# Graph network on one core: in the SAGE rounds, TensorE signals its consumers from drains instead of from the last transpose or product

## What is computed

```python
# block 0: two SAGE layers with normalised rows; block 1: four SAGE layers
agg = segment_sum(h[src], dst); mean = agg / max(count(dst), 1)
h = relu(norm(mean @ W_l + b_l + h @ W_r))      # block 0
h = relu(mean @ W_l + h @ W_r + b)              # block 1
x = layernorm(x + h)                            # after each block
# block 2: attention by edge (GAT); block 3: transformer attention, batch norm
dst = minimum(100000 * uniform ** 2, 99999), sorted
```

## Time and profile before

| what | value |
|---|---|
| median of three executions | 14006.47 us |
| profiled execution, first to last instruction (span) | 16848.3 us |
| mean granted TensorE clock in the profiled execution | 0.667 of full speed |
| TensorE products busy | 8724.5 us, 52% |
| TensorE weight loads busy | 6051.7 us, 36% |
| VectorE busy | 7447.1 us, 44% |
| ScalarE busy | 4895.5 us, 29% |
| GpSimd busy | 7480.4 us, 44% |

### The profile page before, as it was taken

The page is one execution under the profiler, slowest core; times in us unless marked ns, Lnnn a source line. Parts: engine busy times, 40 slices in busy tenths (PEclk is TensorE's granted clock), DMA queues, the critical chain, the costliest instruction groups (busy, mean ns, idle before and its releaser), DMA issues. The chain is left out here.

```text
span 16848.3 us, 221135 instructions
## 1 busy us (share of the span) xinstructions
PE 8724.5 (52%) x38799; PEld 6051.7 (36%) x38898; DVE 7447.1 (44%) x21114; ACT 4895.5 (29%) x11500; POOL 7480.4 (44%) x7460
## 2 busy tenths in 40 slices
PE   6654344533344455445545544454544446677765
PEld 2121233422333344334434433343333323344444
DVE  6654234424454122121112113447888864444456
ACT  0000122223444122122212213344555541222257
POOL 2545554354322654554465455433334336554410
PEclk9775566756666566566656766666666667777776
DMA  6000234424443245345424534554333331233367
GB/s 253 1 3 1 75 120 139 156 71 125 135 143 121 87 148 171 94 126 159 152 88 148 171 97 143 169 190 147 120 121 119 120 113 47 79 98 110 118 193 245
DMA packets 1169327, 2072.17 MB, mean 123 GB/s; under 512 B 283810, under 2 KB 292531, under 8 KB 1156371
## 3 DMA queue, kind: packets, MB, share of 16 engines
q1 hardware_dynamic: 662400, 1128.29, 22.2%
q10 hardware_dynamic: 268534, 564.37, 8.7%
q0 software_dynamic: 238336, 378.92, 8.3%
HBM read 1358.91 MB, written 773.68 MB: 127 GB/s over the span
## 5 line engine op out<-in xcount | busy, mean ns | idle before, releaser
L639 POOL DMA_INDIRECT agg<-y_rows,s_idx x3136 | 3246.2, 1035 | 5507.4 <-ACT y_rows L970 2718.8
L883 PE MATMUL o_bank<-b_parts,ones_parts 3*128 3x512 bf16 (+1 forms) x1568 | 786.2, 501 | 3838.8 <-ACT h_t L1043 2893.0
L886 PE MATMUL o_bank<-w_r,h_t 128*128 128x128 f32 x12544 | 2587.7, 370 | 0.0
L1594 DVE TENSOR_TENSOR total<-o_bank,agg_in 128x512 f32<-128x512 f32 (+1 forms) x1568 | 1048.1, 688 | 3377.2 <-DMA agg_in<-agg 2068.9
L886 PEld LDWEIGHTS o_bank<-w_r,h_t 128*128 128x128 f32 x12544 | 2204.2, 264 | 536.9 <-issue 536.2
L1043 ACT ACTIVATE h_t<-ht_bank 128x512 f32<-128x512 f32 (+1 forms) x1568 | 878.3, 594 | 3930.8 <-remote 2694.1
L883 PEld LDWEIGHTS o_bank<-b_parts,ones_parts 3*128 3x128 bf16 (+1 forms) x1568 | 148.9, 95 | 4192.2 <-ACT h_t L1043 3123.9
L970 ACT ACTIVATE y_rows<-edge_bank,inv 128x128 f32<-128x128 f32 x2352 | 658.7, 373 | 2807.7 <-remote 1640.9
L789 PE MATMUL edge_bank<-w_l,run 128*128 128x128 f32 x4704 | 962.0, 383 | 951.7 <-DVE run L1410 776.4
L630 POOL DMA_INDIRECT gath<-node_a,g_idx x1176 | 1124.9, 957 | 513.6 <-issue 355.1
L630 POOL DMA_INDIRECT gath<-node_x,g_idx x784 | 780.1, 995 | 1079.4 <-PE edge_bank L829 646.1
(11 more groups left out here) (257 smaller groups left out, 14785.5 us busy)
## 6 DMA issues: line engine op xcount, KB each, us to landing
agg_in<-agg SPq DMA_DIRECT2D x1560, 256.0 KB
node_a<-h_out ACTq DMA_DIRECT2D x780, 256.0 KB
h_in<-node_a SPq DMA_DIRECT2D x780, 256.0 KB
node_x<-h_out ACTq DMA_DIRECT2D x392, 256.0 KB
node_b<-h_out ACTq DMA_DIRECT2D x392, 256.0 KB
h_in<-node_x SPq DMA_DIRECT2D x390, 256.0 KB
h_in<-node_b SPq DMA_DIRECT2D x390, 256.0 KB
agg<-zeros ACTq DMA_DIRECT2D x96, 1024.0 KB
```

The costliest lines, as they stand in the source:

```text
L639: pool.indirect_dma_start(agg[order(r)], bass.IndirectOffsetOnAxis(s_idx[q][:, k:k + 1], 0), y_rows[q][:, k, :], None, bounds_check=N - 1, ...
L883: pe.matmul(o_bank[s][0:p, :], ones_parts[:, 0:p], b_parts[:, r, :].unsqueeze(1).to_broadcast([3, RPP, P]), start=True, stop=False, skip_g ...
L886: last = pe.matmul(o_bank[s][0:p, j * P:(j + 1) * P], h_t[s][:, j, 0:p], w_r[r][:], start=False, stop=j == RPP - 1, skip_group_check=True)
L1594: dve.tensor_tensor(flat(total[s], p), o_bank[s][0:p, :], flat(agg_in[s], p), ALU.add).then_inc(sum_ready[s], 1)
```

## The change

In the SAGE rounds the four kinds of TensorE groups (L781, L789, L877 with L886) no longer increment their semaphore with the last transpose or product. A `drain` follows the group, and the drain increments the same semaphore by the same amount. In `front`, which GAT and TR share, the drain is taken only where the kind of the round is SAGE. The short description of the change also says that GpSimd issues all its DMAs without breaks; the diff edits nothing in GpSimd's stream.

```diff
                     for k in range(CPB):
-                        last = pe.transpose(pe_bank[q][:, k * P:(k + 1) * P], gath[q][:, k, :], ident[:])
-                    last.then_inc(gt_ready[q], 1)
+                        pe.transpose(pe_bank[q][:, k * P:(k + 1) * P], gath[q][:, k, :], ident[:])
+                    pe.drain().then_inc(gt_ready[q], 1)
...
-                            last = pe.matmul(pe_bank[2 + q][:, k * P:(k + 1) * P], run[q][:, k * P:(k + 1) * P],
-                                             w_l[r][:], start=True, stop=True, skip_group_check=True)
-                        last.then_inc(yp_ready[q], 1)
+                            pe.matmul(pe_bank[2 + q][:, k * P:(k + 1) * P], run[q][:, k * P:(k + 1) * P],
+                                      w_l[r][:], start=True, stop=True, skip_group_check=True)
+                        pe.drain().then_inc(yp_ready[q], 1)
...
-                        last.then_inc(htp_ready[s], 1)
+                        if kind == SAGE:
+                            pe.drain().then_inc(htp_ready[s], 1)
+                        else:
+                            last.then_inc(htp_ready[s], 1)
...
-                        last.then_inc(mm_ready[s], 1)
+                        if kind == SAGE:
+                            pe.drain().then_inc(mm_ready[s], 1)
+                        else:
+                            last.then_inc(mm_ready[s], 1)
```

More of the change, by code:

```diff
@@ L866, in tr_pair, with front @@
                         tr_values(i + 1, 0)
-                def front(u, r=r, tail=tail):
+                def front(u, r=r, tail=tail, kind=kind):
                     for s in range(2):
```

## The result

The changed kernel takes 15568.38 us (median of 4 executions, 15544.67 to 15590.32), the kernel before in the same measurement 13999.94 us (4 executions, 13985.01 to 14007.88). The ratio is 1.1122 with the interval 1.1106 to 1.1138: slower by 1568 us. The sign is the one forecast, but 14250 and the range up to 14700 are missed by far.

A forecast was written before the change was run, and what follows sets the result against it. No engine is busy above 52%, so waits decide: GpSimd's bursts set the first 35 pairs, units the last 14. Bubbles of 225 us in five rounds and 15 in round 1 make 14006 + 240 = 14246, rounded 14250; range 13880 to 14700.

The forecast's parts named there:

- Two loads that a pair puts side by side: Plain SAGE round: a pair costs the larger of GpSimd's 20.6 us burst and its units; 1130 us a round.
- I therefore take the late signals to be mostly a matter of the recorded execution: TensorE's signals, 15 us late during GpSimd bursts, explain about 2000 of 2842 us between profiled and timed; timed kernel nearly free.
- The bubble: Behind each drained TensorE group the next group moves by 0.35 us (0 to 0.9); 3528 drains, 1235 us on the engine.
- Half on the path: Where units set the pair's time, half of four bubbles counts: 0.7 us a unit, 35 us a round, pairs 10 more.
- TensorE has slack: First 35 pairs, set by GpSimd's bursts: 744 us of TensorE work in over 1000 a round, so nothing charged.
- The clock: TensorE: gaps may lower its clock, product groups then 2.05 us; used only against the lower bubble, no term in the sum.
- the way to 5%: Sign: a timed kernel 5% slower would mean a drain costs far more than a bubble or the clock fell.
- Late signals avoided: Rival, 0.18: TensorE's late signals are real in timed runs and drains go round them; 13750 us or less.
- a span near 15000: Sign in the profile after: span near 15000 us, "remote" before h_t, y_rows and total gone in rounds 0 to 5.
- Lateness inherited: Rival, 0.08: completion itself is late, so TensorE stands still behind drains, idle 10 us and more; 14750 us.
- Nothing measurable: Rival, 0.12: bubbles fall where TensorE waits anyway; only the signal's delay costs, 20 us in all; 14026 us.
- GpSimd "without breaks": GpSimd's instructions are unchanged and it already issues without breaks, 0.30 us between DMAs; this half costs nothing.

The follow-up runs named there:

- own waits: Against the changed kernel: no drains; the last instruction increments and TensorE waits for that increment at all four places; 15136.56 us, ratio 1.0824 to the kernel before.
- units only: Against the changed kernel: drains only behind the h_in transposes and the products with w_r, none on the edges' groups; 18008.95 us, ratio 1.0672 to the kernel before.
- the bare drain: Against the changed kernel: increments back on the last instruction, a drain that signals nothing behind it, all four places; 18610.3 us, ratio 1.1037 to the kernel before.

## Why the prediction missed

**Two loads that a pair puts side by side, the last 14 to 17 pairs set by units: right.** Without late signals the first third runs at GpSimd's pace, 319 us for 16 pairs, changed or not, with own waits or with drains behind the h transposes alone; a plain round takes 1122 us where I had worked out 1130.

**"I therefore take the late signals to be mostly a matter of the recorded execution": wrong.** Timed and profiled executions of one chip agree: a median of 16856.61 us goes with a span of 16862.8 on one, 13989.15 with 13999.1 on another. The page of before and the times shown with it came from chips in different conditions, so the 2842 us between them say nothing of the recording. By luck the consequence was right, since the chip where the result was timed has none: late signals play no part in the ratio.

**The bubble: size about right.** I took 0.35 us for the move of the next group. The rows show gaps of 0.23, 0.32, 0.23 and 0.70 us, 0.37 on the mean, behind the end of a group; with the 0.06 to 0.17 us by which groups overlapped before, the move is nearer 0.5, within my bounds of 0 and 0.9. The load stands behind the end of the group, by 0.20 us in the row shown, as expected. What I had not foreseen is the 0.70 us behind the last group of a unit. It is there with own waits too (0.61 us), so it isn't the drain's. The profile shows no other engine's wait there; the engine's own loop work is my guess and wasn't tested.

**"Half on the path" and "TensorE has slack" in the first 35 pairs: wrong from pair 17 on.** In the second third I charged nothing, and it lost 84 us. In the last third and the tail I charged 45 us, and it lost 229. Units went from 6 to 7 us to 8.84, and I had said about 6.

**The clock: the step that failed.** I wrote "Gaps may lower it" and used that only against the lower bubble, with no term in the sum. It is nearly the whole sum. Busy time of TensorE rises by 1602 us for a loss of 1564. On one chip, drains that left the clock alone cost 50 us; stops at all places brought it from 0.705 to 0.615 and cost 1147 without any drain instruction, with gaps of mostly 0.06 us; with drains, whose gaps are longer, the loss was 424 us more. That stops lower the clock is shown on this chip by two kernels, the changed one and the own wait; which of the stops do it is not. I had the price of the lower level at hand: 2.05 us for a group. I could have asked what a unit costs with every group at it: two of 2.05, two bias products of 0.60 and transposes of 1.91 make some 7 us with no gap at all, against the 5.2 us in which units came at the end of round 2. That would have shown TensorE as the bound before any bubble is charged. The last sentence of the prediction names this as the way to 5%: "that a drain costs far more than a bubble or that the clock fell". The second happened.

How busy TensorE is does not tell the level. In the last third after, TensorE is busy 541.05 of 694 us, 78%, and stands at 0.51; before, it is busy 341.20 of 465, 73%, and stands at 0.82; with own waits it was busy 91% of 32.63 us on end at 0.50. The lower clock lengthens the busy time itself, so a high share is no sign of the higher level. What sets the level no run here shows.

**Late signals avoided: didn't arise in the ratio, and wrong where signals are late.** In units only ScalarE waits up to 28.4 us for a drain, and the kernel is 6.7% slower. My forecast of a span near 15000 and of "remote" waits gone in rounds 0 to 5 but still there in TR compared with the page from a chip with late signals; the profile after has no such wait anywhere, in changed code or not. **Lateness inherited: true on chips that have it**, with stops of up to 12.5 us behind the drains before the transposes and +10.4% for the bare drain. **Nothing measurable: wrong for the change, nearly right for the h transposes alone** (0.38%).

**GpSimd "without breaks":** no edit in the diff, and its busy time is 7479.5 us against 7481.9. It costs nothing, as said.

What stays open: which kinds of drain lower the clock on a chip without late signals, and whether the one at the turn of the loop does most of it; why 1176 drains after transposes leave it alone (after products alone, every trial was with late signals); what brings late signals. Each chip was met in one set only, so whether they belong to the chip or to its state at the time isn't separated. No variant beat the kernel before; the nearest was slower by 0.38%.

## What to carry to other kernels

Leave the increment on the last product of a group. A drain, or a wait of TensorE on its own result, behind each small group (ratios 1.1127 and 1.0824 here) can cost less by its own gap than by the clock: work out the stretch once with every TensorE group at the lower level's duration (here 2.08 us for a group of products that takes 1.16 at the higher), and see whether the engine becomes the bound. One kind alone, behind the h transposes, was nearly free here (50 us), so the price can't be read off one of them. Before reasoning from a difference between a profiled and a timed execution, make sure they are from the same chip: here two chips differed by 20% with the same kernel.

## What the runs showed of the hardware

- Increments on TensorE's instructions arrived late while GpSimd started indirect DMAs (ScalarE waited 16.20 us for one in the earlier trace rows), on some of the chips met and not on others. The same kernel took 16863.16, 16856.34, 16585.06 and 16580.28 us on four chips with it and 13989.15 on one without.
- On a chip with late signals, a bare drain shows the lateness as standstill of TensorE (7.11 us in the rows above, up to 12.5 us before the transposes, against 2.2 at most without late signals). So there it isn't only the other engines that learn of the end late; whether the products themselves ended late, no row tells.
- With drains behind all groups, without late signals, TensorE's mean granted clock was 0.51 or 0.52 of full speed over each whole SAGE round, at a busy share of 56% in round 1 and 70% in the others. In the last two stretches of round 2 it was 0.52 and 0.51, without the drains 0.71 and 0.82 with the same work. Gaps of some 0.06 us between groups and 0.38 to 0.65 us at the end of a unit (own wait, 5926.21 to 5958.84) went with a clock of 0.50 over four units, 91% busy.
- Gaps behind the h transposes alone (0.23 us before the transposes at 5324.15, 0.32 before the bias product at 5333.49 in that kernel), with the products unbroken, left the clock where it was (0.83 in the last stretch, 0.82 without drains).
- A stop by drain cost 0.12 us more than a stop by waiting on the engine's own increment (424 us over 3528).
